# A decoder layer's score stage: halves of a state scan spread over the blocks of maxima, and their first product moved to GpSimd there

## What is computed

```python
scores = jnp.einsum('bhqd,bhkd->bhqk', q, k) / jnp.sqrt(jnp.float32(D))
attn = jax.nn.softmax(scores, axis=-1)
std = jnp.einsum('bhqk,bhkd->bhqd', attn, v)
...
def step(state, xs):
    d_t, B_t, C_t, u_t = xs
    dA = jnp.exp(d_t[..., None] * A)
    state = state * dA + (d_t * u_t)[..., None] * B_t[:, None, :]
    y_t = jnp.einsum('ben,bn->be', state, C_t)
    return (state, y_t)
```

## Time and profile before

| what | value |
|---|---|
| median of three runs | 1685.23 us (1676.9 to 1688.4) |
| the profiled execution | 1676.73 us, its span 1675.0 us |
| VectorE busy | 1271.8 us, 76% |
| TensorE busy | 1240.8 us, 74% |
| GpSimd busy | 441.0 us, 26% |

### The profile page before, as it was taken

The page is one execution under the profiler, slowest core; times in us unless marked ns, Lnnn a source line. Parts: engine busy times, 40 slices in busy tenths (PEclk is TensorE's granted clock), DMA queues, the critical chain, the costliest instruction groups (busy, mean ns, idle before and its releaser), DMA issues.

```text
span 1675.0 us, 13988 instructions
## 1 busy us (share of the span) xinstructions
PE 1240.8 (74%) x4570; PEld 574.9 (34%) x4570; DVE 1271.8 (76%) x1425; ACT 710.5 (42%) x1038; POOL 441.0 (26%) x367
## 2 busy tenths in 40 slices
PE   5564747876977957787986867778786785788696
PEld 4332223323433422233443422333443432333353
DVE  5878978799477887889567895879657896879534
ACT  6674425353363424443363333444363341534221
POOL 1000221012365231102356322001245531101254
PEclk8767968787997878788898788789898797779698
DMA  7753895454245594645235595455135387455122
GB/s 204 263 155 105 189 233 113 101 106 108 71 108 141 121 219 115 127 98 120 71 85 138 124 212 139 89 123 123 57 91 143 88 198 185 88 113 134 34 94 79
DMA packets 108696, 213.87 MB, mean 128 GB/s; under 512 B 13664, under 2 KB 24416, under 8 KB 108624
## 3 DMA queue, kind: packets, MB, share of 16 engines
q1 hardware_dynamic: 89248, 144.95, 30.5%
q0 software_dynamic: 18432, 67.12, 20.7%
q10 hardware_dynamic: 944, 0.92, 0.2%
HBM read 116.08 MB, written 29.62 MB: 87 GB/s over the span
## 4 chain that ended last, share of the span: by engine, by line
DVE 32%; PE 26%; DMA 16%; issue 12%; ACT 2%; POOL 2%; SPq 2%; DVEq 0%; ACTq 0%; POOLq 0%
PE ps L1399 11%; DVE ST L830 10%; PE ps L1369 5%; DMA qk_parts<-PT 5%; DVE ST L824 5%; DMA YA<-ST 5%; DMA GU<-gu_tiles 4%; DVE MX L886 4%; DVE ST L833 3%; PE ps L1207 3%; PE ps L1224 2%; DVE BST L866 2%; SPq L335 1%; DMA KS<-qk_parts 1%; DVE X L876 1%
## 5 line engine op out<-in xcount | busy, mean ns | idle before, releaser
L830 DVE TENSOR_TENSOR_SCAN ST<-dA,ST 128x1024 f32<-128x1024 f32 x128 | 332.9, 2601 | 15.8 <-ACT dA L542 11.6
L437 POOL DMA_DIRECT2D YA<-ST x128 | 111.4, 870 | 788.6 <-DVE ST L833 770.0
L1399 PE MATMUL ps<-V,GU 128*128 128x512 f16 x1024 | 261.0, 414 | 42.8 <-DMA GU<-gu_tiles 37.2
L1207 PE MATMUL ps<-KS,QS 96*128 96x512 f32 x256 | 137.1, 613 | 148.6 <-DVE MX L886 75.7
L886 DVE TENSOR_REDUCE MX<-ps 128x1 f32<-128x512 f32 x256 | 164.9, 685 | 101.4 <-PE ps L1207 101.3
L542 ACT ACTIVATE dA<-DL,Aneg 128x511 f32<-128x511 f32 x256 | 167.7, 713 | 93.2 <-DVE ST L830 93.0
L1369 PE MATMUL ps<-WP,QS 128*128 128x512 f32 x512 | 150.6, 440 | 47.3 <-DVE QS L1016 44.1
L833 DVE TENSOR_TENSOR ST<-ST,BC 128x1024 f32<-128x1024 f32 x128 | 180.6, 1411 | 4.4
L673 ACT ACTIVATE PT<-ps 128x1024 f32<-128x1024 f32 x128 | 125.1, 1019 | 120.3 <-PE ps L1313 119.6
L1399 PEld LDWEIGHTS ps<-V,GU 128*128 128x128 bf16 x1024 | 102.9, 105 | 196.5 <-issue 55.0
L824 DVE TENSOR_TENSOR ST<-DU,BC 128x1024 f32<-128x1024 f32 x128 | 156.2, 1220 | 15.1 <-issue 8.1
(11 more groups left out here) (220 smaller groups left out, 1629.6 us busy)
## 6 DMA issues: line engine op xcount, KB each, us to landing
YA<-ST POOLq DMA_DIRECT2D x128, 512.0 KB, 7.1
BC<-bc_rows SPq DMA_DIRECT2D x64, 512.0 KB, 5.9
qk_parts<-PT SPq DMA_DIRECT2D x64, 256.0 KB, 6.5
GU<-gu_tiles SPq DMA_DIRECT2D x64, 256.0 KB, 3.7
WP<-proj_tiles SPq DMA_DIRECT2D x64, 256.0 KB, 2.7
QS<-qk_parts SPq DMA_DIRECT2D x48, 256.0 KB, 5.5
KS<-qk_parts SPq DMA_DIRECT2D x48, 256.0 KB, 5.8
ST<-in_L_ffn_w_gate_up_dram SPq DMA_DIRECT2D x16, 256.0 KB, 3.4
```

Source lines behind the costliest of these rows:

```text
L830: nc.vector.tensor_tensor_scan(flat, dA[:, a, :, :].rearrange("p e s -> p (e s)"), flat, 0.0, ALU.mult, ALU.add).then_inc(s_scan, 1)
L1207: mm(ps[:, n % 2, :], QS[i][0:3 * D, h, qt * P:(qt + 1) * P], KS[i][0:3 * D, h, :], start=True, stop=True).then_inc(s_xs, 1)
L1399: last = mm(ps[:, f % F_RING, :], GU[:, t % 2, k, m * P:(m + 1) * P], XHL[:, z, k, :], start=(k == 0 and z == 0), stop=(k == KT - 1 and z ...
```

## The change

Three things are changed.

1. For slots 0 to 2 `slot_halves` puts one half at each of `c` = 0, 1, 2 and what is left at `c` = 3. With two or three halves nothing is left; the fourth half of slot 2 in batch 0 stays at `c` = 3. The order of the halves and their number per slot stay. ScalarE's `exp_dA`, SyncE's `load_bc` and GpSimd's transfers follow the same function and move with it.
2. GpSimd makes `dBu` (a 128x1024 product, as L824) for the halves at `r` > 12 of the projection stage and at `c` < 3 of slots 0 to 2: 12 halves in batch 0 and 9 in each of batches 1 to 3, 39 of 128. In its program each stands ahead of the transfer of the half before it. It waits for the product of the half before, for the `BC` load and for the transfer that frees the ring buffer.
3. VectorE leaves L824 out for these halves; its scan waits for `s_dBu`, as before.

```diff
             if j < NG - 1:
-                third = len(mine) // 3
-                return [[], mine[:third], [], mine[third:]]
+                return [mine[0:1], mine[1:2], mine[2:3], mine[3:]]
...
+        def maxima_in_fill(r):
+
+            return r > 3 * KT
+
+        def maxima_in_slot(j, c):
+
+            return j < NG - 1 and c < KT - 1
...
         @block.gpsimd
         def _(pool):
+            def dBu(bb, n, a):
+                g = half(bb, n, a)
+                pool.wait_ge(s_prod, g)
+                pool.wait_ge(s_bc[n % 2], 16 * (DS // 2) * bb + 16 * (n // 2 + 1))
+                n_before, a_before = divmod(g - RING, 2)
+                pool.wait_ge(s_yacc[a_before], 16 * (n_before + 1))
+                nc.gpsimd.tensor_tensor(ST[:, ring(bb, n, a), :, :], DU[:, 2 * a:2 * a + 2, :],
+                                        BC[:, n % 2, 0:1, :].broadcast_to((P, 2, S)), ALU.mult).then_inc(s_dBu, 1)
...
                     for n, a in fill_halves(r, first):
+                        if maxima_in_fill(r):
+                            dBu(b, n, a)
                         add_y_behind(b, n, a)
...
-                    for chunk in slot_halves(j, first):
+                    for c, chunk in enumerate(slot_halves(j, first)):
                         for n, a in chunk:
+                            if maxima_in_slot(j, c):
+                                dBu(b, n, a)
                             add_y_behind(b, n, a)
...
-            def scan_half(bb, n, a):
-
+            def dBu(bb, n, a):
...
+            def scan_half(bb, n, a, made_on_pool=False):
+
+                g = half(bb, n, a)
+                if not made_on_pool:
+                    dBu(bb, n, a)
                 dve.wait_ge(s_dBu, g + 1)
...
-                        scan_half(b, n, a)
+                        scan_half(b, n, a, maxima_in_fill(r))
...
-                            scan_half(b, n, a)
+                            scan_half(b, n, a, maxima_in_slot(j, c))
```

## The result

| | median, us | lowest to highest | ratio to before, 95% interval |
|---|---|---|---|
| before (4 runs) | 1683.9 | 1676.9 to 1688.4 | |
| after (4 runs) | 1714.87 | 1714.36 to 1723.5 | 1.0198 [1.0157, 1.0239] |

The change costs 31 us, 2.0%. The forecast was 1722, slower by over 1% with a chance of 0.80.

What follows compares the result with a forecast made beforehand. Neither VectorE (76% busy) nor TensorE (74%) is full; halves behind a slot's last maximum are hidden by the stack load. +43.8 (batches 1 to 3), +5.1 (batch 0), -6 (transfers) give +43, so 1722 us, 8 in 10: 1695 to 1745.

Steps and rivals of the forecast that it cites:

- A half ahead of the last maximum is paid in full: Score stage: a half ahead of a slot's last maximum delays everything after it, 4.72 us; one behind it is free.
- rival D: GpSimd's dBu takes the upper bound of 4.45 us, +8 to +15, so 1735; chance 0.14.
- Rivals C and E: C: VectorE bounds every slot, 1629, chance 0.06. E: VectorE's and TensorE's waits swap, no effect, 1677 to 1690, chance 0.08.
- The +1.4 for the six maxima: Slot 0, c = 1: TensorE stood still behind the half at c = 0, so the maxima take 5.97 us, not 4.59.
- the +1.2 up to the stack load: Slot 0, batches 1 to 3: last maximum to stack load takes 2.81 us, as in batch 0, instead of 1.62.
- The term of the stack transfers: Stack loads: fewer GpSimd transfers beside them, so they land sooner, -1 us at six places, -6 in all.
- +3.6: Forecast growth from slot 0's last maximum to slot 1's first, over all batches, before the stack transfers' share of -6.
- Rival B: Stack transfers land 2 to 3 us earlier at eight places, no slower block behind c = 0: +23, 1700; chance 0.14.
- Slot 1 (+8.8 before the transfers): Slot 1, all four batches: +3.48 at c = 0, -1.24 at c = 1, stretch behind unchanged; net +2.2 each.
- Slot 2 in batches 1 to 3 (+4.8): Slot 2: +3.48 at c = 0, 0.6 of it replacing a TensorE wait, -1.24 at c = 1; +1.6 each.
- Projection stage (+4.6): Projection step 14: dBu on GpSimd delays two L451, +0.9 in each of batches 1 to 3; +1.9 in batch 0.
- The signs named ahead: After: product near 2.5 us, 39 times; 9 to 12 us waits before slots 1, 2; slot 0 about 33 us.

Runs made afterwards that it cites:

- both profiles: First profile of the changed kernel, and a second from rerunning it unchanged on another chip: 1712.8 us, ratio 1.0183.
- The short-load pair: Stack loads of groups 2 and 3 cut to an eighth of their columns: on the kernel before 1668.22 us, on the changed kernel 1688.01 us.
- the kernel with slot 0 as before: Changed kernel, but slot 0 deals its halves as before (none at c = 0, a third at c = 1, rest at c = 3): 1679.03 us, 0.9998.
- the kernel of the places alone: Kernel before with one half at each of c = 0, 1, 2 of slots 0 to 2, all dBu on VectorE: 1752.58 us, 1.0431.
- with the transfer ahead: Changed kernel with GpSimd issuing the accumulating transfer of the half before ahead of dBu instead of behind it: 1730.35 us, ratio 1.0276.
- three places more: Places of before, GpSimd's dBu at c = 1 and projection steps above 12, plus three halves per batch: 1660.25 us; without the projection steps 1659.73.

## Why the prediction was right, step by step

**Right.** A half ahead of the last maximum is paid in full: slot 0 up to its last maximum was to grow by 30.1 us and grew by 29.9 in both profiles. Its parts fit too: in batches 1 to 3 the half at `c` = 0 costs 3.7 to 3.8 (forecast 3.83), the half and the slower block at `c` = 1 4.92 (4.88). The short-load pair and the kernel with slot 0 as before show that this is the cause. `dBu` takes 2.349 us (2.5 taken from two pieces); rival D, 4.45, is out. VectorE's busy time fell by 40.5 us (48 expected; the scans took 7.0 more, 339.9 against 332.9: five more of them, 48 instead of 43, run beside a subtraction of GpSimd's, all five in the projection stage). Rivals C and E are refuted by the kernel of the places alone, 72 us slower.

**Right in size, cause told in part.** The +1.4 for the six maxima came as 1.46, and the +1.2 up to the stack load as 1.2 in each of batches 1 to 3. They were said to come from TensorE having stood still. The chain shows what stands behind both: in slot 0 the eight products with the values took 1.00 us before (658.57) and 1.87 after (675.79), and the eight instructions ahead of the load 1.55 and 2.73. It is the lower clock, 0.96 down to 0.71. The kernel before shows the price without any half ahead: its blocks at `c` = 1 take 4.59 us in slot 0, at the higher level, and 6.05 in slot 1, at the lower. So the slower block can come without a half at `c` = 0 too, as in batch 2 of the kernel with slot 0 as before, where slot 0 is longer by 2.3 us.

**Wrong sign.** The term of the stack transfers: -1 at six places, as fewer of GpSimd's transfers would run beside them. The landing became longer, 8.06 instead of 7.40 in batch 1 and a median of 6.6 instead of 5.8 over all of `KS`, and SyncE's issues by 0.9. The count of transfers in the window did fall; what counted was that the last one is issued only 1.6 us ahead of the load. Behind slot 0 it makes +12.7 where +3.6, less most of the 6, stood: 3.6 are TensorE's, as forecast, 5.3 the transfers' of batches 1 to 3. In batch 0 the stretch grew by 3.8, and by 3.4 with the transfer ahead and by 4.5 with no product on GpSimd; that part goes with the `BC` load ahead of the stack load, which no term of the forecast has. Rival B, whose case this term was, had it the wrong way round altogether.

**Too large.** Slot 1 (+8.8 before the transfers): at `c` = 0 and 1 it came as forecast, +3.46 and -1.25, but what follows up to slot 2 gave back 1.0 us a batch in the first profile and 1.9 in the second, against "stays as long". Slot 2 in batches 1 to 3 (+4.8): -0.5 and +1.8 in the two profiles. The chain that was level was VectorE's as much as ScalarE's, so the fewer halves behind the last maximum let the end come up to 1.2 us sooner. Projection stage (+4.6): +0.3 and +2.4; its 0.9 for step 14 was taken below the 1.4 that its own working gives.

**The sum.** +43 was expected between the profiled executions, and +45.8 in span came, since the stack transfers (about 12 to 15 too low) and slots 1 and 2 with the projection stage (some 14 too high) cancel. That is luck: two errors of a third of the sum each, with opposite signs. What was not luck is the 30 us of slot 0. Between the medians it is 31: the base of the sum lay 7 us under the median of its kernel, and the profile after 9 us above its own. The forecast had allowed 2 us for the first and could not know the second. The 1722 stands against 1715, with a mechanism that held for the main term.

**The signs named ahead.** Product near 2.5 us, 39 times: yes. A wait of 9 to 12 us ahead of slot 1: 12.1 in batch 0, 15.2 in the others. Ahead of slot 2: no, there it is split, 5.02 us for ScalarE's reciprocals and 1.16 and 0.93 for TensorE. Slot 0 about 33 us: 35.7. Slot 1 longer by 2: 0.3 to 1.2 on average.

## What to carry to other kernels

Ask of each piece of filler whether the chain passes before or behind it: a half behind the last maximum was free, the same half ahead of it cost 3.5 to 4.9 us in slots 0 and 1, and taking a quarter of its work to another engine did not change that. Moving work to an idle engine paid where the filler already stood on the chain (-15 us, and -25 with three places more where VectorE is the bound all through). Before a transfer is issued ahead of one that others wait for, look at when, not at how many; and where an engine is made to wait, count that it comes back slower.

## What the runs showed of the hardware

- With VectorE halves of 3.5 us between its score tiles TensorE's granted clock in slot 0 was 0.71 in batch 1 and 0.79 in batches 2 and 3, against 0.96 and 0.97; a group of eight products went from 1.00 to 1.87 us, a block of six maxima from 4.59 to 6.05. The lower level in that block came in 20 of 20 slots with such a half and in 9 of 32 without. The same kernel has its slot 1 at 0.80 in 34.5 us and at 0.70 in 37.0.
- One accumulating transfer of 512 KB, started by GpSimd 1.6 us ahead of six loads of 256 KB started by SyncE, goes with 1.27 us for one of SyncE's issues and 8.06 for the landing; started 3.1 us ahead, with 0.57 and 6.79. From the first issue to the last landing that is 11.5 us against 9.2.
- GpSimd takes 2.35 us for a 128x1024 product of two fp32 operands, against 1.22 on VectorE. Beside it an instruction of VectorE's with two operands in SBUF took 1.72 us instead of 0.69 for 512 columns; one with an operand in PSUM kept its 0.74, and the maxima their mean of 685 ns in both kernels.
